# A sandwich of mixture-of-experts, state-space mixer and mixture-of-experts: routing of the second expert layer moved into the mixer's pipeline

## What is computed

```
x = x + 0.5 * ffn(layernorm(x))
x = x + mixer_layer(layernorm(x))
x = x + 0.5 * ffn(layernorm(x))

ffn(x):
    shared = (silu(x @ sw1) * (x @ sw2)) @ sw3                 # 128 -> 256 -> 128
    probs  = softmax(x @ rw + rb)                              # 8 experts
    w, idx = top_k(probs, 2); w = w / sum(w)
    h      = silu(x @ ew1[e]) * (x @ ew2[e])                   # every token, its two experts
    return shared + sum over the two experts of w_e * (h @ ew3[e])

mixer_layer(x):
    h   = x + mixer(rmsnorm(x))      # projection, convolution over 4 tokens, SiLU,
                                     # a scan over time with state 4 heads x 64 x 16, gate, projection
    return h + (silu(rmsnorm(h) @ gate) * (rmsnorm(h) @ up)) @ down      # 128 -> 352 -> 128
```

## Time and profile before

| what | us |
|---|---|
| median of three runs | 884.35 (884.25 to 884.9) |
| the profiled execution, its own time | 887.1 |
| its span (first to last instruction) | 885.1 |
| start of the first combine to the mixer's last addition (L1450 at 267.8, L1252 until 601.5) | 333.7 |
| from there to the first tile transpose (L1868 at 723.9) | 122.4 |
| expert tiles of the second layer, until 863.8 | 139.9 |
| combining and storing | 21.3 |

### The profile page before, as it was taken

One profiled execution on the slowest core, in us unless ns is written; L12 is line 12 of the kernel. 1 busy time (PEld: TensorE's weight loads), 2 busy tenths in 40 slices (PEclk: granted clock), 3 DMA queues, 4 the chain that ended last, 5 costly groups with the idle time before them and its releaser, 6 DMA issues.

```text
span 885.1 us, 13651 instructions
## 1 busy us (share of the span) xinstructions
PE 661.0 (75%) x3736; PEld 475.5 (54%) x3736; DVE 557.7 (63%) x1746; ACT 390.8 (44%) x673; POOL 511.9 (58%) x664
## 2 busy tenths in 40 slices
PE   2556679888843589789999999894547789888950
PEld 2234457777741255547667667663224458777840
DVE  5544555454527599898898999945534545454527
ACT  1211224344413989698888887320101124433410
POOL 3867564555554585777966866522866424555550
PEclk9978799999975789799999999996688799999975
DMA  9311122222215000000000000000111122222218
GB/s 276 107 50 46 44 69 74 79 70 73 59 24 188 1 1 1 1 1 1 1 1 1 1 1 2 1 1 10 39 49 46 47 67 71 74 74 77 59 33 273
DMA packets 55512, 46.34 MB, mean 52 GB/s; under 512 B 8456, under 2 KB 51053, under 8 KB 55440
## 3 DMA queue, kind: packets, MB, share of 16 engines
q1 hardware_dynamic: 46736, 28.54, 11.9%
q0 software_dynamic: 8704, 16.93, 5.8%
HBM read 25.30 MB, written 21.19 MB: 53 GB/s over the span
## 4 chain that ended last, share of the span: by engine, by line
PE 45%; another core or an unknown queue 14%; DVE 14%; issue 11%; ACT 8%; POOL 6%; DMA 2%; DVEq 0%; POOLq 0%; ACTq 0%; SPq 0%
PE ps_go L1905 4%; PE ps_go L1549 4%; PE ps_go L1857 3%; PE ps_a L1847 3%; PE ps_go L1894 2%; PE ps_b L1849 2%; PE ps_a L1671 2%; DVE x L1450 2%; PE ps_b L1777 2%; ACT arena L975 2%; POOL xs L678 2%; PE ps_go L1716 2%; PE ps_go L1712 2%; PE ps_b L1883 2%
## 5 line engine op out<-in xcount | busy, mean ns | idle before, releaser
L688 POOL DMA_INDIRECT ys<-arena,dest x144 | 140.8, 978 | 139.9 <-DVE arena L1442 91.7
L678 POOL DMA_INDIRECT xs<-rows,pos x128 | 125.1, 977 | 79.3 <-DVE pos L1362 43.4
L1905 PE MATMUL ps_go<-w_down_e,arena 128*128 x576 | 80.3, 285 | 6.6 <-DVE arena L1442 5.8
L1905 PEld LDWEIGHTS ps_go<-w_down_e,arena 128*128 128x128 f32 x576 | 73.2, 199 | 7.9 <-issue 7.9
L946 ACT ACTIVATE silu_a<-ps_a 128x512 f32<-128x512 f32 x32 | 19.1, 596 | 114.0 <-PE ps_a L1847 45.0
L1894 PE MATMUL ps_go<-ident,hid 128*128 128x128 f32 x288 | 44.0, 275 | 28.5 <-ACT arena L975 26.7
L975 ACT ACTIVATE arena<-ps_go 128x512 f32<-128x512 f32 x72 | 42.9, 596 | 44.5 <-remote 41.0
L1442 DVE COPY arena<-ps_go 128x256 f32<-128x256 f32 x72 | 30.6, 425 | 46.8 <-remote 27.0
L1549 PE MATMUL ps_go<-arena,w_tap 128*128 128x512 f32 x128 | 58.5, 611 | 0.0
L1894 PEld LDWEIGHTS ps_go<-ident,hid 128*128 128x128 f32 x288 | 33.6, 141 | 45.6 <-issue 37.2
L600 POOL TENSOR_TENSOR zs<-zs,us 128x512 f32<-128x512 f32 x16 | 23.0, 1439 | 56.8 <-DVE us L1219 56.8
(11 more groups left out here) (332 smaller groups left out, 1931.3 us busy)
## 6 DMA issues: line engine op xcount, KB each, us to landing
arena<-xs SPq DMA_DIRECT2D x144, 65.0 KB
rows<-ys SPq DMA_DIRECT2D x8, 512.0 KB, 4.1
arena<-ys SPq DMA_DIRECT2D x8, 512.0 KB, 7.9
ys<-arena,dest POOLq DMA_INDIRECT x144
x<-in_L_attn_x SPq DMA_DIRECT2D x8, 256.0 KB, 4.5
arena<-in_L_ffn_ew SPq DMA_DIRECT2D x4, 512.0 KB, 6.4
xs<-rows,pos POOLq DMA_INDIRECT x128
out<-x SPq DMA_DIRECT2D x8, 256.0 KB, 3.9
```

Source lines behind the costliest of these rows:

```text
L678: pool.indirect_dma_start(xs, bass.IndirectOffsetOnAxis(pos[:, n, k * TT + t:k * TT + t + 1], 0), rows[:, n * TT + t, :], None).then_inc(s ...
L688: pool.indirect_dma_start(ys, bass.IndirectOffsetOnAxis(dest[:, i:i + 1], 0), y_out[:, p % YRING, j, :], None, bounds_check=2 * TOK - 1, o ...
L1905: r = pe.matmul(ps_k[:, j * P:(j + 1) * P], hid_t[:, p % 2, at:at + P], w_down_e[:, bass.ds(which[2 * p + j], 1), k, :].rearrange("p a d - ...
```

## The change

Routing of the second expert layer is split at EARLY = 5. Blocks 0 to 4 are routed in the mixer's pipeline: statistics, rows, transposes, logits, choice, ranks, places and row scatters are new steps in the bodies of PE, DVE, ACT and POOL, up to three iterations behind the block's last mixer step, with a buffer `xr` and banks of their own (`rx`, `rl`, `rk`). Behind the mixer `pe_ffn_again` and its three partners run the shared expert of all eight blocks, with the routing of blocks 5 to 7 in its first turns. The placing of C goes from POOL to ACT, `dt_sum` and `angle_in` from DVE to POOL. All bodies of the mixer are put into another order, and the banks are dealt anew, so nearly every `after` is another. The first expert layer keeps its order; of the second, the tiles keep theirs. The diff, cut to its core:

```diff
+EARLY = 5
         pb = {
-            "zt": banks[2], "dt": banks[3], "u": (banks[4], banks[5]), "z": (banks[6], banks[3]),
...
+            "zt": banks[5], "dt": banks[6], "u": (banks[4], banks[6]), "z": (banks[0], banks[7]),
...
+            "rx": banks[3], "rl": banks[0], "rk": banks[7],
+        def early(block):
+            return block if block and SQ * block[0] + block[1] < EARLY else None
+            for n in range(-8, NB + 9):
...
+            def route_rstd(b, q):
+                n = SQ * b + q
+                if n == 0:
+                    pool_rows_again(pool)
+                pool_rstd(pool, ffn_own, NB + n)
+            def route_scatter(b, q, k):
+                pool_scatter(pool, NB + SQ * b + q, (2 * k, 2 * k + 1))
             def body(at):
+                do(bc_conv, at(-3))
+                do(gated_output, at(-5), 1)
+                do(norms, at(-1))
+                do(route_scatter, early(at(-9)), 0)
+                do(route_rstd, early(at(-7)))
+                do(route_scatter, early(at(-9)), 1)
+                do(angle_in, at(-3))
+                do(log_refs, at(-3))
+                do(bc_norms, at(-3))
+                do(c_relative, at(-4))
+                do(tail, at(-5))
+                do(h_norm, at(-5))
+                do(h_add, at(-5))
+                do(route_scatter, early(at(-9)), 2)
+                do(dt_sum, at(-2))
+                do(bc_spread, at(-3))
+                do(route_scatter, early(at(-9)), 3)
+                do(gated_output, at(-4), 0)
...
+                for n in range(EARLY, NB):
+                    pool_rstd(pool, own, NB + n)
+                for n in range(EARLY, NB):
+                    pool_scatter(pool, NB + n)
...
+            def c_places(b, q):
+                act.wait_ge(cf_ready, n + 1)
+                for h in range(NH):
+                    act.activation(cfx[rows_of]..., t6[q][rows_of]..., ACT.Copy).then_inc(cfx_ready, 1)
+        def act_route_xt(act, n, answers):
+            act.wait_ge(rx_ps_ready, n + 1)
+            if n:
+                act.wait_ge(logits_ps_ready, NB + n)
+            act.activation(xr[:, :], answers, ACT.Copy).then_inc(rx_ready, 1)
...
             def body(at):          # DVE
+                do(b_between, at(-4))
+                do(route_stats, early(at(-7)))
...
+                do(route_rows, early(at(-7)))
...
+                do(route_choice, early(at(-8)))
...
+                do(route_places, early(at(-8)))
+                do(ffn_add, at(-6))
...
+        def dve_ffn_again(dve, own):
+            dve.wait_ge(mixer_done, NB)
+            late = range(EARLY, NB)
+            for n in late:
+                dve_stats(dve, own, NB + n)
+            for n in late:
+                dve_norm(dve, NB + n)
+            for n in range(NB + 1):
+                if n < NB:
+                    dve_hid(dve, NB + n, 0)
+                if 1 <= n <= NB - EARLY:
+                    dve_places(dve, own, NB + EARLY + n - 1)
+                if n < NB:
+                    dve_hid(dve, NB + n, 1)
+                if n:
+                    dve_shared(dve, NB + n - 1)
+                if n < NB - EARLY:
+                    dve_route(dve, own, NB + EARLY + n)
+                if n == NB - EARLY:
+                    dve_tiles(dve, own, 1)
...
+        def pe_ffn_again(pe):
+            pe.wait_ge(mixer_done, NB)
+            pe.wait_ge(rank_read, NB + EARLY)
+            pe_xt(pe, NB)
+            pe_xt(pe, NB + 1)
+            for n in range(NB + 1):
+                late = EARLY + n
+                if n < NB:
+                    pe_up(pe, NB + n, 0)
+                if late < NB:
+                    pe.wait_ge(xt_ready, NB + n + 2)
+                    pe_route_xt(pe, late, ps_t)
+                if 0 <= n - 1 < NB - EARLY:
+                    pe.wait_ge(rank_read, NB + late - 1)
+                    pe_rank(pe, NB + late - 1)
+                if n < NB:
+                    pe_up(pe, NB + n, 1)
+                if late < NB:
+                    pe.wait_ge(logits_read, NB + late)
+                    pe_route_logits(pe, late, ps_r)
+                if n + 2 < NB:
+                    if late < NB:
+                        pe.wait_ge(rx_ready, late + 1)
+                    pe_xt(pe, NB + n + 2)
+                if n:
+                    pe_down(pe, NB + n - 1)
+            pe_experts(pe, 1)
```

More of the change, by code:

```diff
@@ L722, in _ @@
             pool_ffn(pool, own, 0)
-            pool_mixer(pool)
+            pool_mixer(pool, own)
             pool_ffn(pool, own, 1)
@@ L1346, in dve_route, with dve_places @@
                               ALU.add).then_inc(chosen_ready, 1)
[L1348 removed]
+        def dve_places(dve, own, turn, answers=ps_k):
             n = turn % NB
@@ L1511, in dve_ffn, with dve_experts @@
+        def dve_experts(dve, own, call):
             dve_gates(dve, own, call)
```

610 lines of the change are left out of this document (319 added, 291 removed).

## The result

The changed kernel takes 855.54 us in the median of four runs (854.65 to 861.2), the kernel before 884.62 beside it: a ratio of 0.9676, 95% interval 0.9626 to 0.9727. 854 was forecast, with a range of 834 to 880. Executions in a slower state of the chip are left out of the ratios and their intervals, not out of the medians and ranges in brackets. The profiled execution took 854.65 us for a span of 852.9.

What follows compares the result with a forecast made beforehand. PE's pace was taken to bound the mixer, and long scatter runs to hold PE in the stage behind it. 887.1 - 48.4 (stage) + 18 (mixer) = 856.7, with the median 2.75 lower: 854 us, range 834 to 880.

Steps and rivals of the forecast that it cites:

- The stage, 74 us: Second FFN's routing and shared expert behind the mixer: 122.4 us become 74, from 61.9 without holds plus 12 of holds.
- (a): Mixer: routing blocks 0 to 4 adds work to PE and DVE, 2.6 us per block, 13 in all, bounds 9.5 and 29.
- (b): Mixer: ACT takes over the four placing instructions and a copy, 3.1 us per routed block, covered by PE, so nothing.
- (c): Mixer: POOL drops placing, gains products, a root and scatters; the scatters go into its idle time, +1 us.
- (d): Mixer: pairs of scatters hold PE for nothing; twelve in a row beside the last block's tail cost 6, 4 on the path.
- (e): Mixer's start: first block's way as long as before, first FFN's combines two iterations sooner; 0, between -5 and +5 us.
- +18: The mixer as a whole gets 18 us longer, range +5 to +38.
- The expert tiles, 0: Second layer's expert tiles, after routing and shared expert: left alone by the change, 140 us as before.
- Lower clock: Rival: stage behind the mixer still gets 0.76 of the clock, +17 us, 871 us in all; chance 0.12.
- No holds: Rival: spaced scatters never hold PE; 62 us for the stage, +13 for the mixer, 838 us in all; chance 0.12.
- Holds everywhere: Rival: every scatter costs PE 0.72 us wherever it stands, in mixer and late stage, +30 us, 884 us; chance 0.07.
- Slower, scatters stretched beside a busy DVE: Rival: busy DVE stretches the mixer's forty scatters, 30 us more by the median ratio, 71 by the worst; chance 0.08.

Runs made afterwards that it cites:

- early0: Changed kernel with EARLY at 0, all eight blocks routed behind the mixer; 898.04 us, ratio 1.0127 to the kernel before.
- scatter_late: Changed kernel with all 64 row scatters behind the mixer, routing of five blocks still in it; 894.54 us, ratio 1.0145 to the kernel before.
- early0_pool: early0 with C placed on POOL again, behind the norms, run on the second chip; 824.14 us, ratio 1.0156 to the kernel before.
- idle_slots: Changed kernel with scatters of blocks 0 to 2 where POOL waits, six in one place and two behind the angles; third chip, 781.41 us, ratio 0.9593.
- after_again: The changed kernel itself, unaltered, measured again on the third chip; 782.47 us, ratio 0.9636 to the kernel before.

## Why the prediction was right, step by step

The total came out within 2 us of the forecast, but part of that is luck: two errors of 8 us in the mixer cancel, and what is left over there, 5.5 us too little, is made up by 6.2 us that were not forecast at all (the tiles 3.8, the start 2.4). The stage behind the mixer, which carries the gain, was right on its own.

**What bounds the kernel.** Right: the mixer went at PE's pace up to the routing, the stage behind it was held by the run of scatters.

**The stage, 74 us: measured 72.9.** Its parts hold as well. The sum without holds was 61.9; without late signals the stage takes 59.6 us, with pauses 60.2. The holds were put at 12; 72.9 less 60.2 is 12.7. The price of 0.5 for each scatter was the right total by a wrong rule, though: the hold is one piece of 12.22 us in a run of sixteen at 1.26 us each, and nothing at 1.81 us. Of the signs named for it one failed: the clock was 0.86 and not over 0.9. With pauses it is 0.94, without late signals 1.00, so the low clock goes with that piece.

**(a) Routing, 13 us: measured 5.2,** below the bound of 9.5 that I gave. The step that failed is "PE gets 1.9 us per block": it took each group from its first start to its last end. In the stage of the changed kernel the next group begins 0.44 us after the transposes, 0.20 after the ranks and 0.80 after the logits:

```profile
634.52 0.60 PE L1938 MATMUL ps_tr<-ident,rows 128*128 128x128 f32 x4
634.96 0.18 PE L1958 MATMUL ps_go<-chosen,earlier 128*128 128x32 bf16 x1
...
635.16 1.10 PE L1971 MATMUL ps_a<-xt,w_shared 128*128 128x512 f32 x2
...
636.97 0.95 PE L1944 MATMUL ps_tr<-rw,xr 128*128 128x8 f32 x8
637.77 0.63 PE L1932 MATMUL ps_tr<-ident,rows 128*128 128x128 f32 x4
```

That is 1.44 per block, 7.2 for five. PE's busy time over the mixer grows by 5.1 us from early0 to scatter_late (296.4 to 301.5, summed over the blocks' windows). DVE's share was put too high as well: routing adds 3.6 us to it (30.88 to 34.45) where 5.3 was forecast, while the two products that it loses were right (32.41 to 30.88, where 1.4 was forecast). The forecast took windows with the short waits in them; their busy time is 4.8. As DVE stays under PE's 36.04, the mutual waits that I added are missing.

**(b) ACT placing, 0:** right. ACT has 35.71 of 37.80 us at most (34.0 was forecast), and early0_pool is no faster.

**(c) POOL +1 and (d) holds +4: measured 12.8.** The tail's hold was 5.4, rightly placed and near in size. The other 7.4 stand against "+1" for scatters that "are put into POOL's idle time". That step asked only who waits for POOL. It did not ask which DVE instruction will now stand beside a scatter and the POOL instruction behind it. The profile had a hint, since 26.8 us of such excess lay in the mixer before. That these instructions make up the 7.4 is likely, not shown: their excess grows by 7.9 us, but idle_slots took it away only in part and left the whole mixer as long.

**(e) Start, 0:** the mixer's first block left 147.5 us after the first combine; before, its end at 419.9 less 267.8 gives 152.1. So 4.6 us were won, inside the bound. But the new order costs later: in early0 the last two blocks (577.9 to 605.4) take 27.5 us against 20.2 before, and the whole mixer 5.5 more.

So +18 came out as +23.5: routing 8 too much, scatters 8 too little, the order's 5.5 missing. The two large errors cancel by luck.

**The expert tiles, 0: measured -3.8.** Not explained. With the same instructions, and counted from the first tile to the first combine, they take 140.5 us before and 139.5 in early0, but 136.1 to 136.7 in the four other kernels of the first chip; PE's signals are late beside the answers' scatters too (64 in the changed kernel, by 2.7 us at most), and what decides between the two lengths was not tried.

**The rivals.** *Lower clock:* 0.86 at least in part, but together with the hold. *No holds* is what the second and third chips do (59.6; by its own terms that rival's time is 837 us, not 838). *Holds everywhere* never came: in the seven blocks of the mixer before the last, where nearly all scatters come in twos, five signals of PE are late, by 1.3 us at most. *Slower, scatters stretched beside a busy DVE:* refuted as put. The forty scatters in the mixer average 1.01 us:

```profile
L694 POOL DMA_INDIRECT xs<-rows,pos x40 | 40.6, 1014 | 10.5 <-issue 10.5
```

against a mean of 0.97 for the 64 beside a half idle DVE in the kernel before. The Trainium skill's rule that was weighed for this rival (SBUF — State Buffer, "SBUF: two separate sides") has POOL wait for DVE. Here it is rather DVE that is held with the scatters in the mixer, by 24.1 us in sum against 16.2.

## What to carry to other kernels

Before moving work to another engine's idle time, list what will then run side by side. Here POOL had the time, but in four places a DVE instruction now began beside a scatter with a POOL product behind it, and one of 0.17 us lasted 2.52. Price small matmuls by the distance of starts, not from start to end. And where a producer issues scatters in long runs, look for results that are read late while nothing is missing, and set the time of the signal beside the end of the instruction. On the chip that shows it, a pause of 1.1 us behind every second scatter gave back 16 us; on one that doesn't, it gives nothing.

## What the runs showed that was not expected

The chips differ by 8% on the same kernel (884.15, 811.87, 812.38 us). Each was used in one sitting only, so chip and sitting cannot be told apart. For the changed kernel, 852.9 and 780.8 us of span, 71.2 of the 72.1 us of difference lie in the stretches in which POOL issues DMAs (first layer 128.1 and 109.0, its tiles 137.3 and 121.8, last block 14.4 and 9.0, the stage 72.9 and 59.6, second tiles 136.1 and 118.2), and the lateness of PE's signals goes with it (175 late signals on the first chip, none on the others), while blocks of the changed kernel's mixer agree (34.2 and 34.3 us, 37.8 and 37.8, 40.5 and 40.5, 38.9 and 39.7). Slower transfers are not the reason: the packets of POOL's DMA queue take 51.9 us of the 16 DMA engines on the one and 51.8 on the other, and POOL's 272 DMA instructions sum to 266.9 and 268.1 us. The Trainium skill (SBUF — State Buffer, "SBUF: two separate sides") says that PE and ACT never wait on anyone at the engine ports. The second and third chips agree, with 1.11 us in after_again where the first has 12.22. The first chip's hold need not contradict it: it depends on the distance of scatters in time, leaves the instructions' own times as they are and delays only their signals, nearly all of them PE's. What it is stays open.
